# A graph network on one core: the attention sum fetches each visited tile's queries, and the experts' weights are split there instead of in the message sum

## The chip, the cores and the metric

The kernel runs on 1 core of a Trainium2 chip. The metric is the device time of one execution in microseconds (us). Times are compared as medians of several runs.

## The reference, cut to what matters

The model is two layers over 3125 nodes with 256 features and 50,000 edges (sorted by destination). A layer adds a message sum over the graph, a mixer and a feed-forward block, and layer 1 has an attention over the edges. The two parts that matter here:

```
# layer 0: messages along the edges (a scaled sum per destination node)
x = x + gnn(xn, W, edges) + mix(xn)
# layer 1: attention over the edges, 8 heads of 32
q = feat @ Wq.T + bq;  k = feat @ Wk.T + bk;  v = feat @ Wv.T + bv
score = clip(sum(q[edge_dst] * k[edge_src]) / sqrt(32), -10, 10)      # per edge and head
alpha = softmax of score over the edges of one destination
wv = segment_sum(alpha * v[edge_src], edge_dst)
# end of layer 1: a shared expert and 8 routed ones (top 2 of 8)
shared = gelu(x @ W1s + b1s) @ W2s + b2s
priv   = gelu(x @ W1p[e] + b1p[e]) @ W2p[e] + b2p[e]
```

The experts' weights W1p (8 x 256 x 1024), W2p (8 x 1024 x 256), W1s and W2s are float32. The kernel uses them as two float16 halves, a high one and the rest, which it makes itself and keeps in DRAM (`wsplit`) until the expert stage at the end.

## The kernel before, in words

The program is a row of phases with a barrier of all engines behind each (`phase`, L105 and L115). The nodes are 25 tiles of 125 rows (`T`, `R`). The edges are 80 groups of 5 x 125 (`G`, `J`). As the edges are sorted by destination, a group touches only one to a few node tiles; each (group, tile) pair is a *visit*, and `group_table` tells every engine the first tile, the number of tiles and the number of visits before a group (`group_bounds`, L522).

**Message sum** (`message_sum`, L686). For each group GpSimd issues 5 indirect DMAs (L750), each of which gathers 125 source rows of 1 KB (two float16 halves) into one of 4 slots. For each visit VectorE builds a one-hot matrix (L773), TensorE sums the gathered rows into the tile with it (L811), and VectorE adds the sum to the node tile (`Adder.add`, L557). VectorE also copies the next group's indices for GpSimd (L784). Two jobs ride along. The `Turner` transposes other weights in five parts. The `Splitter` (L628) works through 18 half-experts: SyncE issues two loads of 512 KB (L660), ScalarE makes the high float16 halves (L676), VectorE the low ones (L681, after every second group, for the first 18 of 20 turns of the loop), and SyncE stores two results of 512 KB (L664).

**Attention sum** (`attention_sum`, L1632). At its start SyncE issues one load of all queries, 3.2 MB, into the buffer of `m.y` (L1705), and then, for each group, a load that spreads the group's 625 destination numbers over 125 partitions, 312.5 KB (L1709), two buffers ahead. GpSimd gathers, per group, 5 x 125 rows of 2 KB (key and value, L1689) into one of 5 slots. For each visit ScalarE makes one-hot columns (L1736, L1742), four visits ahead at most (`PICKS`), and TensorE picks each edge's query out of the tile with 10 matmuls (L1784, between three that clear and three that close the bank, L1775 and L1788). VectorE multiplies queries and keys and reduces them to scores (L1822, L1827, L1828), ScalarE takes the exponential (L1749), VectorE weighs the values (L1834) and builds the one-hots of the sum (L1866), TensorE sums (L1810), VectorE adds to the tile (L555). TensorE picks for group n+2 before it sums group n. After the loop VectorE waits for the last gathers and divides by the sums (L1878 to L1883).

The order on each engine is the program's, written out by hand; semaphores tie the engines. SyncE and ScalarE each have a DMA queue of their own for the loads and stores they issue, GpSimd has the one of the gathers.

Of the kernel before, what the change touches and what calls it, by code (L numbers as in the profile page):

```python
# [25 lines left out]
C = 256  # L26
CB = C // 128
R = 125
# [599 lines left out]
class Splitter:  # L628
# [20 lines left out]
    def move(self, sp, e, h):  # L649

        i = e * 2 + h
        source, at = (self.shared, h) if isinstance(e, int) else (self.own, i)
        for s in range(2):
            sp.wait_ge(self.s_whole[s], i + AHEAD)
# [5 lines left out]
            sp.dma_start(to, taken).then_inc(self.s_raw[s], 16)  # L660
        rows = self.m.wsplit[:, :, 0:WALL].rearrange("e p (k l h n) -> e p k l h n", k=2, l=2, h=2)
        for s in range(2):
            sp.wait_ge(self.s_whole[s], i + 1 + AHEAD)
            sp.dma_start(rows[bass.ds(e, 1), :, :, s, h, :].rearrange("e p k n -> p (e k) n"),  # L664
                         self.split[:, s, :, :].rearrange("p k n -> p (k n)").bitcast(F32)
                         .rearrange("p (k n) -> p k n", k=2)).then_inc(self.s_stored[s], 16)

    def finish(self, sp):
        for s in range(2):
            sp.wait_ge(self.s_stored[s], self.steps * 16 + AHEAD)  # L670
# [15 lines left out]
def message_sum(nc, m, a):  # L686
# [6 lines left out]
    with phase(nc, "ms") as ph:  # L693
# [11 lines left out]
        splitter = Splitter(nc, m, a, ph)  # L705
        splitter.s_pace = s_pace
        PARTS = 5
        each = G // SLOTS // PARTS
        whole = splitter.steps

        def stretches(part):

            lo, hi = part * each, (part + 1) * each
            cuts = sorted({lo, hi, *([whole] if lo < whole < hi else [])})
            return list(zip(cuts, cuts[1:]))

        with nc.Block() as block:

            @block.sync
            def _(sp):  # L720
                with sp.Fori(0, X8) as e:
                    for h in range(2):
                        splitter.move(sp, e, h)
                for h in range(2):
                    splitter.move(sp, X8, h)
                splitter.finish(sp)

# [28 lines left out]
            def _(dve):  # L756
# [7 lines left out]
                def groups(i, splits):  # L764

                    for s in range(SLOTS):
# [18 lines left out]
                        if splits and s % 2:  # L785
                            splitter.low(dve, i, s // 2)
                    return before + count

                with dve.Fori(0, whole) as i:
                    groups(i, True)  # L790
                with dve.Fori(whole, G // SLOTS) as i:
                    visits = groups(i, False)
                adder.finish(dve.snap(visits), s_pace)
# [838 lines left out]
def attention_sum(nc, m, dst):  # L1632
# [9 lines left out]
    with phase(nc, "as") as ph:  # L1642
# [10 lines left out]
        q16 = m.y[:, :, :].rearrange("p t c -> p (t c)").bitcast(F16).rearrange("p (t k c) -> p t k c", t=T, k=2)  # L1653
# [6 lines left out]
        zeros = ph.sb("zeros", [R, R], F16)  # L1660
# [4 lines left out]
        summed = ph.sb("summed", [R, T, W])  # L1665
# [9 lines left out]
        ph.ahead(s_pick, *[s_total, s_added] * LAG)  # L1675
        ph.ahead(*[s_pickv] * PICKS)
        with nc.Block() as block:
# [25 lines left out]
            @block.sync  # L1703
            def _(sp):
                sp.dma_start(q16.rearrange("p t k c -> p t (k c)"),  # L1705
                             m.gather_q.rearrange("(t p) n -> p t n", p=R)).then_inc(s_q, 16)

                def load(g, s):
                    sp.dma_start(dsts[:, s, :],  # L1709
                                 dst[bass.ds(g * (J * R), J * R)].unsqueeze(0).broadcast_to([R, J * R]))\  # L1710
                        .then_inc(s_dst[s], 16)

                for s in range(2):
                    load(s, s)
# [5 lines left out]
                for g in range(G, GP):  # L1720
                    sp.wait_ge(s_dfree, g - 1)
                    load(g - G, g % 2)

            @block.scalar
            def _(act):
# [30 lines left out]
                one_hots(2, 1, 0, group_bounds(act, m, 2))  # L1756
                with act.Fori(0, G // (2 * SLOTS)) as i:
                    for s in range(2 * SLOTS):
                        n = i * (2 * SLOTS) + s
                        bounds = group_bounds(act, m, n + 3)  # L1760
                        weights(n + 1, (s + 1) % SLOTS)
                        one_hots(n + 3, i * SLOTS + (s + 3) // 2, (s + 3) % 2, bounds)

            @block.tensor
            def _(pe):
                def pick_q(g, bounds):
# [5 lines left out]
                    anything = q16[:, 0, :, :].rearrange("p k c -> p (k c)")  # L1772
                    for b in range(3):
                        n = min(512, J * C - b * 512)
                        pe.matmul(picked[:, b, 0:n], zeros[:, :], anything[:, 0:n], start=True, stop=False)  # L1775
                    with pe.Fori(0, count) as k:
                        visit = pe.snap(before + k)
                        tile = pe.snap(nc.s_assert_within(first + k, 0, T - 1))
                        pe.wait_ge(s_pick, visit + 1 + AHEAD)
                        pe.sem_inc(s_pace, 1)  # L1780
                        for j in range(J):
                            at = j % 2 * C
                            for p in range(2):
                                ins = pe.matmul(picked[:, j // 2, at:at + C], pick[:, visit % PICKS, j * R:(j + 1) * R],  # L1784
                                                q16[:, tile, p, :], start=False, stop=False)
                        ins.then_inc(s_pickv, 1)
                    for b in range(3):
                        ins = pe.matmul(picked[:, b, 0:1], zeros[:, :], anything[:, 0:1], start=False, stop=True)  # L1788
                    ins.then_inc(s_picked, 1)

                pe.wait_ge(s_q, 16)
# [23 lines left out]
            def _(dve):  # L1815
# [1061 lines left out]
def graph_layers(nc, a, out):  # L2877
    m = Memory()
    with ExitStack() as stack:
# [83 lines left out]
        attention_sum(nc, m, a["dst"])  # L2963
# [25 lines left out]
```

## Time and profile before

| | |
|---|---|
| median of 3 runs | 3982.84 us (3981.74 to 3984.69) |
| the profiled execution | 3987.43 us, its span 3985.7 us |
| busy: PE, DVE, ACT, POOL | 65%, 54%, 32%, 33% |
| mean granted TensorE clock | 0.807 of full speed |
| moved by DMA | 373 MB, mean 94 GB/s |
| message sum | from 235 to 889 us of the span |
| attention sum | from 2369 to 3133 us of the span |

In the profile PE is TensorE, DVE is VectorE, ACT is ScalarE, POOL is GpSimd and SP is SyncE; PEld is the loading of TensorE's weights. A name like SPq is the engine's instruction queue, which issues DMAs. "Idle before" is the time in which an engine did nothing ahead of an instruction, with what ended it; "issue" means that nothing the profile shows was waited for. "DMA share" is the mean busy share of the core's 16 DMA engines, so a transfer that keeps 4 of them busy shows as 0.25.

### The profile page before, as it was taken

Reading aid. Unit: us, or ns where it says so; the run is one execution under the profiler, and the core shown is the slowest. Engines: PE = TensorE matmul, PEld = TensorE weight load, DVE = VectorE, ACT = ScalarE, POOL = GpSimd, SP = SyncE. Lnnn points to the kernel's source line nnn. Section 1 sums busy time; section 2 is a strip of 40 time slices with the busy share of each in tenths; the row PEclk is TensorE's granted clock in tenths of the full one; section 3 lists DMA queues with packets and bytes.
Section 4 is the critical chain, followed back from the end, with each engine's and each line's share of the span. In section 5 each row is a group of like instructions: output and inputs, shape, how many; then the busy total and the mean of one; then the engine's idle time right before and its main releaser. Section 6 shows DMA issues by size and latency. Waiting matters only on the chain. (4 is left out here: it accounts for less than half of the span.)

```text
span 3985.7 us, 66521 instructions
## 1 busy us (share of the span) xinstructions
PE 2587.3 (65%) x17122; PEld 2086.2 (52%) x17123; DVE 2170.5 (54%) x4408; ACT 1269.1 (32%) x2467; POOL 1315.5 (33%) x1017
## 2 busy tenths in 40 slices
PE   4413333436678699996375434777777487699997
PEld 4413333323367477774254423555555366589986
DVE  6523333322456388885237764777777555544445
ACT  0300010003143255553257732222222243345441
POOL 0048888853000000000001024888888500211115
PEclk9855555557679599997597767999999778699998
DMA  1046666730000000001200015777777200356643
GB/s 36 32 105 157 156 165 162 197 94 6 0 22 0 16 11 13 16 16 46 73 0 0 0 40 150 193 189 187 189 191 189 52 21 0 124 188 229 227 159 91
DMA packets 255391, 373.00 MB, mean 94 GB/s; under 512 B 119009, under 2 KB 180889, under 8 KB 250965
## 3 DMA queue, kind: packets, MB, share of 16 engines
q0 software_dynamic: 154752, 174.53, 18.2%
q1 hardware_dynamic: 87700, 185.50, 14.2%
q10 hardware_dynamic: 12864, 12.06, 1.1%
q8 instruction: 37, 0.61, 0.1%
q14 instruction: 38, 0.30, 0.0%
HBM read 320.09 MB, written 50.96 MB: 93 GB/s over the span
## 5 line engine op out<-in xcount | busy, mean ns | idle before, releaser
L750 POOL DMA_INDIRECT ms_got<-gather,ms_index x400 | 506.2, 1265 | 124.9 <-issue 114.4
L1689 POOL DMA_INDIRECT as_gkv<-gather_kv,as_index x340 | 462.0, 1359 | 108.7 <-issue 100.9
L811 PE MATMUL ms_total<-ms_got,ms_hot 125*125 125x256 f16 x1040 | 231.0, 410 | 376.8 <-DMA ms_got<-gather,ms_index 251.9
L811 PEld LDWEIGHTS ms_total<-ms_got,ms_hot 125*125 x1040 | 202.9, 219 | 405.0 <-issue 405.0
L2097 POOL MEMSET bm_fx<- 128x128 f32 x1 | 0.2, 205 | 1013.0 <-POOLq L115 1013.0
L1810 PE MATMUL as_total<-as_gkv,as_hot 125*125 125x264 f32 x850 | 218.8, 406 | 78.0 <-DVE as_summed L555 65.6
L1478 ACT ACTIVATE ex_h<-ex_up,ex_now 128x313 f32<-128x313 f32 (+1 forms) x320 | 196.1, 613 | 197.2 <-PE ex_up L458 190.0
L1810 PEld LDWEIGHTS as_total<-as_gkv,as_hot 125*125 125x125 f32 x850 | 157.7, 193 | 117.8 <-issue 91.8
L2791 DVE CAST moe_hidden<-moe_h 128x256 f16<-128x256 f32 (+1 forms) x336 | 101.8, 303 | 209.9 <-ACT moe_h L2728 209.3
L2728 ACT ACTIVATE moe_h<-moe_up,moe_w 128x256 f32<-128x256 f32 (+1 forms) x336 | 163.1, 487 | 135.2 <-PE moe_up L458 93.2
L1784 PE MATMUL as_picked<-y_rows,as_pick 125*125 x1060 | 150.3, 291 | 52.6 <-issue 47.7
L2680 PE MATMUL moe_down<-moe_w,moe_hidden 128*128 128x256 f16 x1536 | 178.1, 273 | 0.0
L458 PE MATMUL moe_up<-moe_cols,moe_w 128*128 128x256 f16 x1536 | 172.9, 273 | 1.4 <-ACT moe_cols L2735 1.4
L1784 PEld LDWEIGHTS as_picked<-y_rows,as_pick 125*125 x1060 | 123.9, 141 | 87.3 <-issue 84.5
L2567 POOL DMA_INDIRECT moe_rows<-gather,moe_taken x64 | 63.0, 984 | 309.9 <-PE moe_turned L2655 259.8
L676 ACT ACTIVATE ms_split<-ms_raw 128x1024 f16<-128x1024 f32 x36 | 37.6, 1054 | 390.8 <-DMA ms_raw<-in_L_ffn_W1p 350.0
L1520 DVE TENSOR_TENSOR ex_h<-ex_h 128x313 f16<-128x313 f32 (+1 forms) x320 | 155.4, 486 | 11.0
L458 PEld LDWEIGHTS moe_up<-moe_cols,moe_w 128*128 128x128 f16 x1536 | 150.2, 98 | 19.0 <-issue 1.6
L2680 PEld LDWEIGHTS moe_down<-moe_w,moe_hidden 128*128 128x128 f16 x1536 | 150.4, 98 | 17.3
L1866 DVE SCALAR_TENSOR_TENSOR as_hot<-row_no,as_node,edge_dst 125x625 f32<-125x625 f32 x104 | 90.6, 871 | 120.5 <-issue 61.7
L2793 DVE TENSOR_TENSOR moe_hidden<-moe_h,moe_hidden 128x256 f16<-128x256 f32 (+1 forms) x336 | 148.3, 441 | 11.6
L458 PE MATMUL ex_down<-ex_w,ex_h 128*125 128x256 f16 x1200 | 148.1, 276 | 2.3
(448 smaller groups left out, 5895.2 us busy)
## 6 DMA issues: line engine op xcount, KB each, us to landing
moe_w<-wsplit SPq DMA_DIRECT2D x34, 2052.0 KB
as_dsts<-in_dst SPq DMA_DIRECT2D x83, 305.2 KB
wsplit<-ms_split SPq DMA_DIRECT2D x36, 512.0 KB
ms_raw<-in_L_ffn_W1p SPq DMA_DIRECT2D x16, 512.0 KB
ms_raw<-in_L_ffn_W2p SPq DMA_DIRECT2D x16, 512.0 KB
results<-moe_made SPq DMA_DIRECT2D x32, 256.0 KB, 8.2
ms_got<-gather,ms_index POOLq DMA_INDIRECT x400
gather_kv<-qkv_out SPq DMA_DIRECT2D x5, 1250.0 KB
```

Of the source, the lines that this page charges most:

```text
L458: ins = pe.matmul(out, left(k, b), right(n, b), start=(i == 0), stop=(i == len(todo) - 1))
L750: pool.indirect_dma_start(out=got[:, s, j, :], out_offset=None, in_=m.gather0, in_offset=bass.IndirectOffsetOnAxis(ap=index[:, s, j:j + 1] ...
L811: ins = pe.matmul(total[:, visit % RING, 0:C], hot[:, visit % RING, j, :], got[:, s, j, p * C:(p + 1) * C], start=(j + p == 0), stop=(j + ...
L1478: act.activation(h32[:, u % 4, 0:n], up[:, u % 4, 0:n], ACT.Relu, bias=now[:, 1, layer, o:o + 1], scale=now[:, 0, layer, o:o + 1]).then_in ...
L1520: dve.tensor_tensor(to[:, 1, o, at:at + n], full, to[:, 0, o, at:at + n], ALU.subtract).then_inc(s_h, 1)
L1689: pool.indirect_dma_start(out=gkv[s][:, j, 0:2 * C], out_offset=None, in_=m.gather_kv, in_offset=bass.IndirectOffsetOnAxis(ap=index[:, s, ...
L1784: ins = pe.matmul(picked[:, j // 2, at:at + C], pick[:, visit % PICKS, j * R:(j + 1) * R], q16[:, tile, p, :], start=False, stop=False)
L1810: ins = pe.matmul(total[:, visit % RING, 0:W], hot[:, s, j, :], gkv[s][:, j, C:C + W], start=(j == 0), stop=(j == J - 1))
L2680: ins = pe.matmul(down[:, h, 0:C], hidden[:, k, f, h * 128:(h + 1) * 128], part(s, r, 1, f, 0, C), start=False, stop=(f == FB - 1 and n == 2))
L2728: act.activation(h32[:, u % 4, 0:n], up[:, u % 4, 0:n], ACT.Gelu, scale=1.0 / WS, bias=bias(s, f)).then_inc(s_h32, 1)
L2791: dve.tensor_copy(hidden[:, 0, f, at:at + n], full).then_inc(s_hhigh, 1)
L2793: dve.tensor_tensor(hidden[:, 1, f, at:at + n], full, hidden[:, 0, f, at:at + n], ALU.subtract).then_inc(s_hidden, 1)
```

## The change

The queries are no longer loaded at the start. SyncE now walks the visits and, for each, waits until the fetch before it has landed and the slot is free, and then loads the visited tile's queries, 125 rows of 1 KB, into a ring of four (`queries`). TensorE waits for that load ahead of a visit's ten matmuls. The freed buffer takes the attention's running sums, so `m.y` becomes a view with a row of 264 elements in place of 256. The `Splitter` leaves the message sum: SyncE's program there is empty, and ScalarE and VectorE have no split work. In the attention sum ScalarE issues the loads and stores and makes the high halves at five points of its 10-group loop, VectorE makes two low halves after every fifth group, and the two half-steps of the shared expert follow after the loops. The diff, cut to its core:

```diff
-    def move(self, sp, e, h):
+    def load(self, act, e, h):
...
+    def store(self, act, e, h):
+        i = e * 2 + h
...
-            @block.sync
-            def _(sp):
-                with sp.Fori(0, X8) as e:
-                    for h in range(2):
-                        splitter.move(sp, e, h)
-                for h in range(2):
-                    splitter.move(sp, X8, h)
-                splitter.finish(sp)
-                    for lo, hi in stretches(part):
-                        if hi <= whole:
-                            with act.Fori(lo, hi) as i:
-                                for s in range(2):
-                                    splitter.high(act, i, s)
...
-                        if splits and s % 2:
-                            splitter.low(dve, i, s // 2)
...
-        q16 = m.y[:, :, :].rearrange("p t c -> p (t c)").bitcast(F16).rearrange("p (t k c) -> p t k c", t=T, k=2)
+        q16 = ph.sb("q16", [R, PICKS, 2, C], F16)
...
-        summed = ph.sb("summed", [R, T, W])
+        summed = m.y_wide
+        splitter = Splitter(nc, m, a, ph)
...
-                sp.dma_start(q16.rearrange("p t k c -> p t (k c)"),
-                             m.gather_q.rearrange("(t p) n -> p t n", p=R)).then_inc(s_q, 16)
...
+                def queries(g):
+                    first, count, before = group_bounds(sp, m, g)
+                    with sp.Fori(0, count) as k:
+                        visit = sp.snap(before + k)
+                        tile = sp.snap(nc.s_assert_within(first + k, 0, T - 1))
+                        sp.wait_ge(s_q, visit * 16 + AHEAD)
+                        sp.sem_inc(s_pace, 1)
+                        sp.wait_ge(s_pickv, visit + 1)
+                        sp.sem_inc(s_pace, 1)
+                        sp.dma_start(q16[:, bass.ds(visit % PICKS, 1), :, :].rearrange("p a k c -> p (a k c)"),
+                                     m.gather_q[bass.ds(tile * R, R), :]).then_inc(s_q, 16)
                 with sp.Fori(0, G // 2 - 1) as i:
                     for s in range(2):
+                        queries(i * 2 + s)
                         sp.wait_ge(s_dfree, i * 2 + (s + 1))
                         load(i * 2 + (s + 2), s)
...
+                splits = {0: lambda e: splitter.load(act, e, 0), 2: lambda e: high(e, 0),
+                          4: lambda e: (splitter.store(act, e, 0), splitter.load(act, e, 1)),
+                          6: lambda e: high(e, 1), 8: lambda e: splitter.store(act, e, 1)}
+                def high(e, h):
+                    for k in range(2):
+                        splitter.high(act, e * 2 + h, k)
...
+                        if s in splits:
+                            splits[s](i)
+                for h in range(2):
+                    splitter.load(act, X8, h)
+                    high(X8, h)
+                    splitter.store(act, X8, h)
+                splitter.finish(act)
...
-                        tile = pe.snap(nc.s_assert_within(first + k, 0, T - 1))
+                        pe.wait_ge(s_q, visit * 16 + (16 + AHEAD))
...
-                                                q16[:, tile, p, :], start=False, stop=False)
+                                                q16[:, visit % PICKS, p, :], start=False, stop=False)
...
+                        if s == 3:
+                            for k in range(2):
+                                splitter.low(dve, i, k)
                 adder.finish(dve.snap(before + count), s_pace)
+                for h in range(2):
+                    for k in range(2):
+                        splitter.low(dve, X8 * 2 + h, k)
...
-            m.y = y_stack.enter_context(nc.sbuf_tensor(f"y_rows{turn}", [R, T, C], F32))
+            m.y_wide = y_stack.enter_context(nc.sbuf_tensor(f"y_rows{turn}", [R, T, C + X8], F32))
+            m.y = m.y_wide[:, :, 0:C]
```

## Rows read from the trace of the kernel before

**Rows 1.** Page, part 4: the chain that ended last, by line, shares of the span.

```profile
PE moe_up L458 5%; PE moe_down L2680 4%; PE moe_down L2642 1%; DVE moe_hidden L2793 1%; DVE x_rows L2829 0%; DVE moe_hidden L2791 0%; PE moe_turned L2655 0%; PE moe_down L2675 0%; POOL z_rows L2577 0%; DMA moe_w<-wsplit 0%; DVE z_rows L2809 0%; DMA z_rows<-results,place 0%; DVE rowvec L2806 0%; PE moe_down L2694 0%; DVE x_rows L2820 0%
```

**Rows 2.** Groups by line, GpSimd, 237 to 872 us: count, busy, mean, idle before.

```profile
L750 POOL DMA_INDIRECT ms_got<-gather,ms_index x400 | 506.2, 1265 | 124.9 <-issue 114.4 <-DVE ms_index L784 7.6 <-DVE ms_index L761 2.9
```

**Rows 3.** Groups by line, GpSimd, 2435 to 3115 us.

```profile
L1689 POOL DMA_INDIRECT as_gkv<-gather_kv,as_index x320 | 437.7, 1368 | 102.3 <-issue 94.6 <-DVE as_index L1840 7.8
L1689 POOL DMA_INDIRECT z_flat<-gather_kv,as_index x80 | 110.2, 1377 | 63.9 <-DVE as_index L1840 39.7 <-issue 24.2
```

**Rows 4.** Line 750's instructions: duration min, median, max; the low halves' groups.

```profile
L750 POOL DMA_INDIRECT ms_got<-gather,ms_index x400: 1206/1214/2237, 237.6 to 864.5; - x134
...
L681 DVE SCALAR_TENSOR_TENSOR ms_split<-ms_raw,ms_split 128x1024 f16<-128x1024 f32 x36 | 44.1, 1226 | 3.8 <-ACT ms_split L676 3.1
```

**Rows 5.** Timeline, attention sum's start, all engines: start, length, [idle before].

```profile
2368.82 0.29 SPq L1705 DMA_DIRECT2D y_rows<-gather_q  x1
2398.97 1.21 POOL L1689 DMA_INDIRECT as_gkv<-gather_kv,as_index  x1 [0.31 <-issue]
2422.08 1.32 PE L1775 MATMUL as_picked<-y_rows,as_zeros 125*125 125x512 f16 x3 [63.12 <-DMA y_rows<-gather_q]
2424.78 0.82 ACT L1736 ACTIVATE z_flat<-as_dsts,as_minus_node 125x625 bf16<-125x625 int32 x1 [59.69 <-DMA as_dsts<-in_dst]
2429.91 1.49 DVE L1822 TENSOR_TENSOR z_flat<-as_picked,as_gkv 125x1280 f32<-125x1280 f32 x1 [51.61 <-PE as_picked L1788]
```

**Rows 6.** Windows: stretch, its length, busy of five engines, clock, DMA share, GB/s.

```profile
2373.00:2400.00 27.00, 0.00 (x0) 0.00 (x0) 4.88 (x2) 0.00 (x0) 21.64 (x18) 0.50 0.82 203
2408.00:2419.00 11.00, 0.00 (x0) 0.00 (x0) 0.00 (x0) 0.00 (x0) 0.00 (x0) 0.50 0.34 115
2500.00:3000.00 500.00, 357.07 (x1921) 271.13 (x1920) 374.46 (x454) 139.98 (x213) 406.47 (x297) 0.98 0.75 190
300.00:363.00 63.00, 21.89 (x100) 19.23 (x99) 20.18 (x33) 4.23 (x4) 51.07 (x40) 0.58 0.57 145
810.00:860.00 50.00, 17.95 (x80) 15.88 (x80) 13.46 (x25) 0.00 (x0) 39.91 (x34) 0.53 0.34 85
755.00:775.00 20.00, 8.53 (x40) 6.80 (x41) 2.86 (x5) 3.79 (x5) 16.02 (x14) 0.59 1.07 295
```

**Rows 7.** DMA issues of the whole span: count and KB (1024 bytes) of each.

```profile
as_dsts<-in_dst SPq DMA_DIRECT2D x83, 305.2 KB
...
y_rows<-gather_q SPq DMA_DIRECT2D x1, 3125.0 KB
```

**Rows 8.** Instructions of line 1784: ten matmuls for each visit.

```profile
L1784 PE MATMUL as_picked<-y_rows,as_pick x1060: 272/273/446, 2427.2 to 3101.2; 125*125 x177
```

**Rows 9.** Waits of VectorE and ScalarE in the attention sum: total, times, longest.

```profile
DVE z_flat L1822 <- DMA as_gkv<-gather_kv,as_index: 20.1, 13, 3.5
ACT as_gkv L1749 <- DVE as_score L1828: 320.8, 64, 8.2
```

**Rows 10.** Timeline, message sum: one half-step's issue, landing and halves.

```profile
584.95 0.37 SPq L660 DMA_DIRECT2D ms_raw<-in_L_ffn_W1p  x1
591.97 1.06 ACT L676 ACTIVATE ms_split<-ms_raw 128x1024 f16<-128x1024 f32 x1 [26.23 <-DMA ms_raw<-in_L_ffn_W1p]
594.42 1.06 ACT L676 ACTIVATE ms_split<-ms_raw 128x1024 f16<-128x1024 f32 x1 [1.39 <-DMA ms_raw<-in_L_ffn_W2p]
```

**Rows 11.** Timeline, the end of the attention sum.

```profile
3107.31 0.43 DVE L555 TENSOR_TENSOR as_summed<-as_summed,as_total  x1 [2.85 <-PE as_total L1810]
3113.10 1.21 POOL L1689 DMA_INDIRECT as_gkv<-gather_kv,as_index  x1 [0.31 <-issue]
3121.01 0.36 DVE L1878 TENSOR_SCALAR as_gkv<-as_summed 125x200 f32<-125x200 f32 x1 [13.27 <-DMA as_gkv<-gather_kv,as_index]
```

**Rows 12.** Timeline, attention sum at the full clock and at the low one.

```profile
2440.77 2.48 PE L1810 MATMUL as_total<-as_gkv,as_hot 125*125 125x264 f32 x10
3102.76 4.17 PE L1810 MATMUL as_total<-z_flat,as_hot 125*125 125x264 f32 x10 [1.18 <-DVE as_hot L1866]
```

More of the change, by code:

```diff
@@ L659, in move, with finish @@
                 to = self.raw[:, 1, :].rearrange("p (b n) -> p b n", n=C)
-            sp.dma_start(to, taken).then_inc(self.s_raw[s], 16)
+            act.dma_start(to, taken).then_inc(self.s_raw[s], 16)
+    def store(self, act, e, h):
+        i = e * 2 + h
         rows = self.m.wsplit[:, :, 0:WALL].rearrange("e p (k l h n) -> e p k l h n", k=2, l=2, h=2)
         for s in range(2):
[L663 to L668, printed above, removed]
+            act.wait_ge(self.s_whole[s], i + 1 + AHEAD)
+            act.dma_start(rows[bass.ds(e, 1), :, :, s, h, :].rearrange("e p k n -> p (e k) n"),
+                          self.split[:, s, :, :].rearrange("p k n -> p (k n)").bitcast(F32)
+                          .rearrange("p (k n) -> p k n", k=2)).then_inc(self.s_stored[s], 16)
+    def finish(self, act):
         for s in range(2):
-            sp.wait_ge(self.s_stored[s], self.steps * 16 + AHEAD)
+            act.wait_ge(self.s_stored[s], self.steps * 16 + AHEAD)
     def high(self, act, i, s):
@@ L704, in message_sum @@
         turner = Turner(nc, m, a, ph)
-        splitter = Splitter(nc, m, a, ph)
-        splitter.s_pace = s_pace
         PARTS = 5
         each = G // SLOTS // PARTS
[L709 to L715, printed above, removed]
-        with nc.Block() as block:
-            @block.sync
-            def _(sp):
-                with sp.Fori(0, X8) as e:
-                    for h in range(2):
-                        splitter.move(sp, e, h)
-                for h in range(2):
-                    splitter.move(sp, X8, h)
-                splitter.finish(sp)
+        with nc.Block() as block:
             @block.scalar
@@ L762, in _ @@
                 adder = Adder(nc, dve, "ms", m.x, total, s_total, s_added, m.inv_sqrt_degree)
-                def groups(i, splits):
+                with dve.Fori(0, G // SLOTS) as i:
                     for s in range(SLOTS):
@@ L784, in groups @@
                         dve.tensor_copy(index[:, free, :], nxt).then_inc(s_index, 1)
-                        if splits and s % 2:
-                            splitter.low(dve, i, s // 2)
[L787 to L793, printed above, removed]
+                adder.finish(dve.snap(before + count), s_pace)
             @block.tensor
@@ L1674, in attention_sum @@
         s_hot, s_total, s_added, s_pace, s_v = (ph.sem(x) for x in ("hot", "total", "added", "pace", "v"))
-        ph.ahead(s_pick, *[s_total, s_added] * LAG)
+        splitter.s_pace = s_pace
+        ph.ahead(s_pick, s_q, *[s_total, s_added] * LAG)
         ph.ahead(*[s_pickv] * PICKS)
@@ L1720, in _ @@
                 for g in range(G, GP):
+                    queries(g - 2)
                     sp.wait_ge(s_dfree, g - 1)
                     load(g - G, g % 2)
+                queries(GP - 2)
             @block.scalar
@@ L1771, in pick_q @@
                         pe.sem_inc(s_pace, 1)
-                    anything = q16[:, 0, :, :].rearrange("p k c -> p (k c)")
                     for b in range(3):
                         n = min(512, J * C - b * 512)
-                        pe.matmul(picked[:, b, 0:n], zeros[:, :], anything[:, 0:n], start=True, stop=False)
+                        pe.matmul(picked[:, b, 0:n], zeros[:, 0:R], zeros[:, 0:n], start=True, stop=False)
                     with pe.Fori(0, count) as k:
                         visit = pe.snap(before + k)
-                        tile = pe.snap(nc.s_assert_within(first + k, 0, T - 1))
+                        pe.wait_ge(s_q, visit * 16 + (16 + AHEAD))
+                        pe.sem_inc(s_pace, 1)
                         pe.wait_ge(s_pick, visit + 1 + AHEAD)
@@ L1784, in pick_q @@
                                 ins = pe.matmul(picked[:, j // 2, at:at + C], pick[:, visit % PICKS, j * R:(j + 1) * R],
-                                                q16[:, tile, p, :], start=False, stop=False)
+                                                q16[:, visit % PICKS, p, :], start=False, stop=False)
                         ins.then_inc(s_pickv, 1)
                     for b in range(3):
-                        ins = pe.matmul(picked[:, b, 0:1], zeros[:, :], anything[:, 0:1], start=False, stop=True)
+                        ins = pe.matmul(picked[:, b, 0:1], zeros[:, 0:R], zeros[:, 0:1], start=False, stop=True)
                     ins.then_inc(s_picked, 1)
-                pe.wait_ge(s_q, 16)
                 pe.wait_ge(s_zero, 2)
@@ L2962, in graph_layers @@
         take_y(1)
[L2963 removed]
+        attention_sum(nc, m, a)
         attention_out(nc, m)
```

7 lines of the change are left out of this document (4 added, 3 removed).

## The prediction

> **What bounds the kernel now.** I read first the chain of waits, then each changed stage by itself. The chain that ended last [rows 1] lies in the expert stage, which the change doesn't touch; every stage ends at a barrier, so what the two changed stages gain or lose goes straight into the time.
>
> The message sum is bound by GpSimd issuing gathers. 400 of them take 1265 ns and sit idle 125 us in all, nearly all "issue" [rows 2]: 506 + 125 = 631 of the 635 us from 237 to 872. The transfers, ScalarE and VectorE have room.
>
> The attention sum looks the same: from 2435 to 3115 GpSimd issues 400 gathers in 437.7 + 110.2 + 102.3 + 63.9 = 714 us, and of its idle time only 39.7 + 7.8 us wait for an index, 39.7 of it once, at the start [rows 3]. Without that it is 674 us for 80 groups, 8.43 us per group. The reader is to keep the second question open, though: how near to full are the DMA engines, and which of them?
>
> **The change part by part.**
>
> *Split work out of the message sum.* SyncE, ScalarE and DMA weren't late there, so only what slows GpSimd's issue counts. A gather's median is 1214 ns against a mean of 1265 [rows 2, 4]: 0.051 x 400 = 20 us is lengthening. The 36 low halves (44 us of VectorE, 1226 ns each) and 91 us of one-hots are what it can come from. None or all of the 20 us could be the halves'; I take half, a gain of 10 us.
>
> *The start of the attention sum.* The load of all queries is issued at 2368.8 and TensorE starts at 2422.1; VectorE's first scores come at 2429.9, while GpSimd has been out of slots since 2400.2 [rows 5]. With one tile to fetch behind two small loads I put VectorE's first scores near 2385: 45 us earlier, and GpSimd's stall of 39.7 us goes.
>
> *The fetches and the splits as traffic.* This is the term that decides. From 2408 to 2419 nothing but the query load runs, with a backlog, and the DMA share is 0.34 at 115 GB/s [rows 6]: 0.34 x 16 = 5.4, about five of the 16 engines. The load of destination numbers that is issued right behind it reaches ScalarE only at 2424.8, after 59.7 us of waiting [rows 5]: it stood in the queue of the same five. From 2373 to 2400, with gathers beside the load, the share is 0.82, or 13 engines, so gathers use the other engines too, and I spread them evenly. All loads into 125 partitions on SyncE's queue then fall on one set of five engines: the load of destination numbers, and the new fetches.
>
> By the Trainium skill ("DMA: Bandwidth & Descriptors", "Why a DMA increments its semaphore by 16 and not by 1") a load from SyncE or ScalarE uses the largest number of engines up to 16 that divides its rows, and always the lowest-numbered; 125 rows give 5. The trace's 5.4 agrees, and by the rule the fetches speak against this change.
>
> Work on each of those five, in us:
> - a gather. Three readings. At the start 20 gathers put 20 x 5/16 = 6.25 on an engine, taking five engines for each; the query load of 3.2 MB [rows 7] needs 3200/115 = 27.8 us alone and took 53.3; less an estimated 4 for issue and landing, 21.5/6.25 = 3.4. In the message sum's last turns 0.34 x 50 x 16 / 34 / 5 = 1.6 for rows half as long, so 3.2. In the steady attention sum 0.75 x 500 x 16 = 6000 engine-us, less 59 loads of destinations x 13.5, over 297 gathers and five: 3.5 [rows 6]. I take 3.3.
> - a load of destinations: 312.5 KB at 115 GB/s, 2.7.
> - a fetch: 1/25 of 3.2 MB, 1.11, once per visit; there are 1060/10 = 106 visits [rows 8], 1.3 per group.
> - a half-step of the split, 2.1 MB over all 16 engines: the share is 0.57 with it and 0.34 without [rows 6], and 63 us hold two, so 0.23 x 63 / 2 = 7.2.
>
> Per group the five carry 5/16 x 5 x 3.3 + 2.7 = 7.9 us now, 93% of 8.43: nearly full, though the mean share is 0.75. VectorE already waits 20.1 us for gathers [rows 9]. After: 7.9 + 1.3 x 1.11 + 7.2/5 = 10.7 us per group. The whole stage: 131 x 3.3 + 83 x 2.7 + 106 x 1.11 + 16 x 7.2 = 433 + 224 + 118 + 115 = 890 us. Busy shares count waiting too: the mean reaches 1.07 where three queues run [rows 6], so 890/1.07 = 832 is the lower bound of this sum. I take 850, nearer to it, as this stage will also have three queues. The last gather lands at 2371 + 850 = 3221, not at 3121.
>
> *Instructions added.* ScalarE gets 32 high halves of 1.06 us and 64 issues of about 0.4; it idles 320.8 us on scores, 5.0 per group [rows 9], and hides them. A landing late for the high half stops its exponentials, and VectorE behind them; it has two groups to land, about 17 us, against 7.0 and 9.5 in the message sum [rows 10]. VectorE gets 32 low halves, 39 us; they hide under its waits for transfers. If the DMA weren't late they would show (rival A). SyncE waits for one landing per visit; behind it stand only the next destinations, two groups ahead.
>
> *The tail.* After the last add, at 3107.3, VectorE now waits 13.7 us for the last gathers, then divides from 3121.0 [rows 11]. The shared expert's two half-steps go there. ScalarE starts the first about 4 us before the last add; each takes 9.5 for landing [rows 10], 1.1, 1.2 and about 0.7 of semaphores, 12.5; so the division starts 25 - 4 = 21 us after the last add. The last add comes 13.7 us ahead of the last landing, at 3207; the division starts at 3228: 107 us later than before. If the landings cost nothing the tail costs 0, and 12 if they take half as long again.
>
> **The sum.** 3987.4 (the profiled execution; span 3985.7) - 10 + 107 = 4084. That execution is 4.6 above the median, so 4080. With 810 to 890 us of work: 4040 to 4120.
>
> **Rivals.**
>
> *A: the engines interleave better than they were charged, and GpSimd stays the bound: faster.* For it: the gathers kept 1214 ns with a backlog at the start, the steady stage waits little for transfers. Against: the 3.2 to 3.5 us come from three places. GpSimd: -39.7 for the stall, +11 for the low halves (400 gathers at 1.370 against 1.214 are 62 us long already [rows 3]; 32 of 36 halves cost what I took off above; 0 to 39), +10 for the coupling, as VectorE's chain gets as long: 3107.3 - 2429.9 - 20 + 39 + 5 = 701 from 2385 is 3086, and GpSimd's end is 3114.3 - 39.7 + 11 = 3086. The tail adds 21 - 13.7 = 7, the message sum gives 10: -22, so 3961. It decides if the five engines' work is below about 715 us (3086 less 2371), which by the same count needs a gather of 2.3 us: (715 x 1.07 - 457)/131.
>
> The Trainium skill ("SBUF — State Buffer", on the bandwidth-pool intuition) gives 358 GB/s from HBM to a core. By that the stage, at 190 + 50 + 20 = 260 GB/s of demand, would not be bound by transfers, which is A's time; 190 is the trace's, and no run here shows this stage at 358.
>
> *B: the fetches are late by their own order.* The next is issued only when the last has landed, and stands behind 2.7 us of destinations. If each of the 26 second visits of a group shows 2 us, on A's ground: -22 + 52, 4013. For it: a wait in the chain of every visit; against: SyncE is two groups ahead.
>
> *C: on top of the forecast TensorE loses its clock.* It runs at 0.98 in the steady stage and at 0.5 to 0.6 in the message sum [rows 6], where it is 35% busy. With groups of 850/84 = 10.1 us it falls from 71% to 59% busy. A sum of ten matmuls takes 4.17 in place of 2.48 [rows 12]; at half speed TensorE needs 6.0 x 1.7 = 10.2 us per group, as long as the transfers; coupled, 30 to 60 more, 4120.
>
> **Chances.** Forecast 60%, A 22%, B 10%, C 8%. The range holds the forecast, B, C in part and A's edge: 3962 to 4135; the likeliest's own is 4040 to 4120. A measurement of this kernel tells 0.2%, 8 us, from no change. Faster: A but for its slow side, 21%. Within: 5%. Slower: 74%.
>
> **What would show it.** The message sum about 625 us long, with gathers at 1.24. VectorE's first scores near 2375, the message sum's 10 us included. Groups of about 10.1 us in the attention sum, GpSimd idle for indices by over 100 us, VectorE and TensorE waiting for gathers and fetches, a DMA share of about 0.8 at 215 GB/s. Wrong if GpSimd's idle time there is still nearly all "issue", or if a stage of over 760 us shows no wait for a transfer.

## The result: slower, and by more than the range allowed

| | before | after |
|---|---|---|
| median | 3982.6 us (3981.7 to 3984.7, 4 runs) | 4160.3 us (4157.5 to 4162.2, 4 runs) |
| ratio | 1 | 1.0445 [1.0427, 1.0463] |
| profiled execution | 3987.4, span 3985.7 | 4162.2, span 4160.5 |

Forecast: 4080, range up to 4135. The sign and the cause named, late transfers in the attention sum, came out as predicted. The size is 80 us short, and the time lies 25 us outside the range.

### The profile after

The page, parts 4 and 5 (the chain's engines; groups with their count, busy time, mean, and idle time before them):

```profile
PE 11%; DVE 2%; DMA 0%; POOL 0%; issue 0%; ACT 0%; DVEq 0%; POOLq 0%; ACTq 0%
...
L1663 POOL DMA_INDIRECT as_gkv<-gather_kv,as_index x340 | 470.9, 1385 | 291.2 <-DVE as_index L1843 200.0
L730 POOL DMA_INDIRECT ms_got<-gather,ms_index x400 | 498.9, 1247 | 125.1 <-issue 111.5
...
L1788 PE MATMUL as_picked<-as_q,as_pick 125*125 x1060 | 186.3, 339 | 212.4 <-DMA as_q<-gather_q 175.3
```

The chain still lies in the expert stage [rows 1] and says nothing about the change. The message sum's 400 gathers fell from 1265 to 1247 ns [rows 2]: 7 us, where 10 were forecast. In the attention sum the kind of wait has changed: GpSimd, which sat idle on indices for 39.7 + 7.8 us [rows 3], now waits 200.0 us for them, and TensorE, which waited for queries only once before, at the start, waits 175.3 us for fetches.

The waits of the attention sum after, 2364 to 3300 us (total, times, longest):

```profile
ACT as_gkv L1737 <- DVE as_score L1831: 454.8, 64, 18.6
...
POOL as_gkv L1663 <- DVE as_index L1843: 200.0, 42, 14.9
PE as_picked L1788 <- DMA as_q<-gather_q: 175.3, 44, 12.7
DVE as_hot L1869 <- PE as_total L1813: 130.2, 24, 14.6
DVE z_flat L1825 <- PE as_picked L1792: 110.6, 22, 14.1
...
DVE z_flat L1825 <- DMA as_gkv<-gather_kv,as_index: 21.4, 5, 11.1
```

SyncE's own longest wait, in the same stretch, is the one for the landing of the last fetch:

```profile
SPq L1694 <- DMA as_q<-gather_q: 513.7, 99, 13.2
```

Read from the transfer upwards: a fetch is late for TensorE (175), so the picked queries are late for VectorE (111), so the score is late for ScalarE (455 against 320.8 [rows 9]), so slots come free late and GpSimd has no index (200). VectorE hardly waits for gathers: 21.4 us, and 9.9 in the slots that the trace calls `z_flat`, against 20.1 and 3.4 before. So it is the fetches that were late, and not the gathers.

A window after (busy of PE, PEld, DVE, ACT, POOL, then granted clock, DMA share, GB/s), and the last add, the shared expert's low halves and the division on VectorE:

```profile
2500.00:3000.00 500.00, 315.43 (x1451) 247.79 (x1452) 303.90 (x363) 125.68 (x183) 314.26 (x226) 0.82 0.79 196
```

```profile
3270.10 0.43 DVE L555 TENSOR_TENSOR y_rows<-y_rows,as_total  x1 [1.13 <-PE as_total L1813]
...
3293.03 1.22 DVE L684 SCALAR_TENSOR_TENSOR as_split<-as_raw,as_split 128x1024 f16<-128x1024 f32 x1 [7.32 <-ACT as_split L679]
...
3295.61 0.35 DVE L1887 TENSOR_SCALAR as_gkv<-y_rows 125x200 f32<-125x200 f32 x1
```

Against [rows 6]: 226 gathers in the 500 us instead of 297, at nearly the same share and rate, 0.79 and 196 GB/s against 0.75 and 190. The division starts at 3295.6 instead of 3121.0 [rows 11], 174.6 later; from there to the span's end it is 864.9 us in place of 864.7. The whole loss lies ahead of the division.

One number per kernel carries the experiments: the time from the first to the last reduction of a score on VectorE. It contains neither the stage's start nor its tail. In the trace before and the trace after:

```profile
L1827 DVE TENSOR_REDUCE as_score<-z_flat x81: 1485/1486/1489, 2431.4 to 3098.9; 125x40 f32<-125x1280 f32 x81
```

```profile
L1830 DVE TENSOR_REDUCE as_score<-z_flat x81: 1486/1486/1487, 2383.6 to 3263.4; 125x40 f32<-125x1280 f32 x81
```

667.5 us before, 879.8 after. In the kernel before, 20 gathers are already issued when the scores begin; a kernel that starts early without the change takes 690 (below). Each length comes from one trace. The traced execution lies up to 9 us from its kernel's median (e1), so differences of lengths are good to some 10 us, and no better.

### The profile page after: what moved, and what is told of

It is laid out like the page before. It is cut to its first block and busy times, and to the rows that moved or that the text cites. A ratio compares the mean times of both kernels' runs of the same rounds, so it can differ in the third digit from the quotient of the medians.

```text
span 4160.5 us, 68233 instructions
## 1 busy us (share of the span) xinstructions
PE 2662.4 (64%) x17122; PEld 2157.0 (52%) x17123; DVE 2171.8 (52%) x4408; ACT 1266.3 (30%) x2467; POOL 1314.5 (32%) x1017
## 5 line engine op out<-in xcount | busy, mean ns | idle before, releaser
L1663 POOL DMA_INDIRECT as_gkv<-gather_kv,as_index x340 | 470.9, 1385 | 291.2 <-DVE as_index L1843 200.0
L730 POOL DMA_INDIRECT ms_got<-gather,ms_index x400 | 498.9, 1247 | 125.1 <-issue 111.5
L1788 PE MATMUL as_picked<-as_q,as_pick 125*125 x1060 | 186.3, 339 | 212.4 <-DMA as_q<-gather_q 175.3
L1813 PE MATMUL as_total<-as_gkv,as_hot 125*125 125x264 f32 x850 | 254.4, 455 | 53.5 <-DVE y_rows L555 49.0
L1788 PEld LDWEIGHTS as_picked<-as_q,as_pick 125*125 x1060 | 156.6, 169 | 245.4 <-issue 242.8
L1813 PEld LDWEIGHTS as_total<-as_gkv,as_hot 125*125 125x125 f32 x850 | 183.8, 226 | 101.8 <-issue 64.9
L616 ACT ACTIVATE ms_cols<-ms_bank 128x256 f32<-128x256 f32 (+2 forms) x26 | 11.7, 449 | 671.2 <-PE ms_bank L603 647.5
L1825 DVE TENSOR_TENSOR z_flat<-as_picked,as_gkv 125x1280 f32<-125x1280 f32 x65 | 96.7, 1488 | 121.7 <-PE as_picked L1792 100.2
L752 DVE SCALAR_TENSOR_TENSOR ms_hot<-row_no,ms_node,edge_dst 125x625 f32 x104 | 90.7, 872 | 133.1 <-issue 133.1
```

Source lines behind the costliest of these rows:

```text
L730: pool.indirect_dma_start(out=got[:, s, j, :], out_offset=None, in_=m.gather0, in_offset=bass.IndirectOffsetOnAxis(ap=index[:, s, j:j + 1] ...
L1663: pool.indirect_dma_start(out=gkv[s][:, j, 0:2 * C], out_offset=None, in_=m.gather_kv, in_offset=bass.IndirectOffsetOnAxis(ap=index[:, s, ...
L1813: ins = pe.matmul(total[:, visit % RING, 0:W], hot[:, s, j, :], gkv[s][:, j, C:C + W], start=(j == 0), stop=(j == J - 1))
L1825: dve.tensor_tensor(qk[:, :].rearrange("p (j c) -> p j c", j=J), picked[:, :, :].rearrange("p b c -> p (b c)")[:, 0:J * C] .rearrange("p ( ...
```

## The experiments

Each stands beside runs of the kernel before on its chip; brackets are 95% intervals of the ratio. "Length" is the score-to-score time of its trace.

| run | what it is | ratio | first score | length |
|---|---|---|---|---|
| e1 | fetches; splits in the message sum | 1.0132 [1.0073, 1.0192] | 2395.9 | 766.9 |
| e2 | after; destinations on ScalarE's queue | 1.0529 [1.0497, 1.0562] | 2374.9 | 923.5 |
| e3 | after; fetch of 128 rows | 1.0339 [1.0309, 1.0369] | 2377.2 | 842.4 |
| e4 | after; destinations into 128 rows | 1.0383 [1.0353, 1.0413] | 2371.5 | 866.1 |
| e5 | after; two groups' fetches under way | 1.0462 [1.0441, 1.0483] | 2375.0 | 890.5 |
| e6 | e1; two groups' fetches under way | 1.0152 [1.0132, 1.0173] | 2398.6 | 764.0 |
| e7 | before; queries in five pieces | 0.9975 [0.9965, 0.9985] | 2391.2 | 697.2 |
| e8 | after; e3 and e4 | 1.0244 [1.0222, 1.0266] | 2376.2 | 799.4 |
| e9 | before; fetches that nobody reads | 1.0223 [1.0197, 1.0248] | 2431.5 | 758.5 |
| e10 | e1; thin fetches | 0.9964 [0.9948, 0.9981] | 2389.9 | 706.0 |
| e11 | before; destinations into 128 rows | 0.9992 [0.9982, 1.0002] | 2434.5 | 659.3 |
| e12 | e7 and e11 | 0.9963 [0.9947, 0.9979] | 2397.7 | 690.8 |
| e13 | after; thin fetches | 1.0282 [1.0264, 1.0301] | 2378.2 | 826.4 |
| e14 | after; thin splits | 1.0247 [1.0219, 1.0276] | 2406.7 | 791.1 |
| e15 | after; both thin | 1.0101 [1.0079, 1.0124] | 2401.9 | 733.4 |
| e16 | before; pieces spread out | 0.9969 [0.9957, 0.9981] | 2389.7 | 690.3 |

### Is it the fetch, the split, or the order of the queue?

*e1, one half of the change.*

```diff
+ (message sum)   splitter.move / high / low, as in the kernel before
- (attention sum) splitter.load / high / low / store
```

> The splits go back into the message sum as before; the attention sum keeps the fetch of each tile's queries. Theory W (the five DMA engines that serve loads into 125 partitions have too much work; the changed kernel's stage took about the 890 us that the plain sum gives): the splits' 115 us leave those five engines and the tail's 12 us go, the message sum gets its 7 us back: about 4040 us. Theory O (each fetch waits for the landing of the last, and stands behind the destinations in one queue; the engines aren't full): the splits ride on another queue, so the fetches hardly get faster: above 4110 us.

4035.2 us, beside the 4040 of theory W. The fetch costs 52 net of the earlier start; moving the splits costs the other 125.

*e2, order alone: the destinations leave SyncE's queue.*

```diff
-    sp.dma_start(dsts[:, s, :], ...)       # between the fetches
+    act.dma_start(dsts[:, s, :], ...)      # behind the square that frees the slot
```

> The changed kernel with the loads of destination numbers issued by ScalarE on its own queue, right after the one-hots that free the buffer; SyncE's queue holds only the fetches. The same bytes on the same five engines. Theory W: no change, 4145 to 4170 us. Theory O: a fetch no longer stands behind 2.7 us of destinations, 106 times, so TensorE's waits for queries fall by more than half of their 175 us: below 4080 us.

4193.3, slower still. TensorE waits 190.2 us for fetches instead of 175.3, though nothing stands ahead of a fetch in its queue. The place behind the destinations isn't the cause.

*e5 and e6, the wait of one fetch for the last one's landing.* SyncE waited 513.7 us at that wait in the trace after, so it had to be tried.

```diff
-    s_q = ph.sem("q")
+    s_q = [ph.sem(f"q{s}") for s in range(2)]     # by the group's parity
...
+                    with pe.Fori(count, MOST) as k:       # TensorE's program, for each group: MOST is 4
+                        pe.sem_inc(s_q[par], 16)
```

> The changed kernel with one semaphore for each parity of the group, so that the fetches of two neighbouring groups may be under way together; the same bytes, buffers and queues. Theory C (new, from the four runs before: the stage is a chain of 106 fetches, each issued when the last has landed; in the changed kernel and the four runs a visit takes the fetch's time from issue to last byte plus 1.0 to 1.5 us): the chain opens, the stage falls to what bounds it next, 4000 to 4080 us. Theory W (the five engines are full): the same bytes take the same time, 4150 us or more.

> The splits in the message sum as before, the fetches of two groups under way together. Theory C: with the chain open the stage is bound by GpSimd's issue again and starts 45 us earlier: 3940 to 3965 us. Theory W: the five engines carry 775 us of work against about 715 us of issue by GpSimd: 4020 to 4040 us, as with one fetch at a time.

4166.8 and 4043.6: nothing gained, on either base. But the edit also puts a loop of semaphore instructions into TensorE's program, between a group's last pick and the matmuls that close its bank. TensorE's waits in e1, then in e6, 2362 to 3310 us:

```profile
PE as_picked L1799 <- DMA as_q<-gather_q: 111.7, 44, 6.5
```

```profile
PE as_picked L1807 <- issue: 78.3, 67, 1.5
...
PE as_picked L1801 <- DMA as_q<-gather_q: 29.6, 13, 4.8
```

TensorE's wait for fetches fell by 82 us, and 78 us came up ahead of the closing matmuls, where e1 has none. In e5 it is 99.4 in place of 175.3, and 62.9 new. So the two runs took one wait away and put about as much in, and they don't show that the wait was free. That each fetch waits for the last one's landing stays a possible part of the cost.

### Is it the traffic, or waiting for it?

*e9 has the traffic without TensorE's wait for it, e10 every wait without most of the traffic.* In e9 SyncE still waits for each landing, and the next destinations are issued behind it.

```diff
e9 (from before)
+    sp.dma_start(idle[:, visit % PICKS, ...], m.gather_q[tile * R : ...])   # never read
e10 (from e1)
-    sp.dma_start(q16[...],          m.gather_q[tile * R : ..., :])
+    sp.dma_start(q16[...][:, 0:64], m.gather_q[tile * R : ..., 0:64])
```

> The kernel before, queries held whole and splits in the message sum, and beside it each visit's fetch of 125 rows into a scratch ring that nobody reads: the traffic of the fetches without TensorE's wait for them. Theory W (the five engines' work): 118 us more on each of the five, no earlier start: 4070 to 4100 us. Theory D (what costs is that TensorE waits for a fetch): 3980 to 3995 us.

> As the first of these experiments (fetches in the attention sum, splits in the message sum), but each fetch takes only 64 of a row's 512 elements; the rest of the queries is left out (zero). Every wait, issue and landing stays, an eighth of the bytes. Theory W: the five engines carry about 680 us, GpSimd's issue bounds the stage and it starts 45 us earlier: 3940 to 3970 us. Theory D: 4025 to 4045 us, as with the whole rows.

4082.6 and 3978.9. Unread fetches lengthen the stage from 667.5 to 758.5, 91 us. The same fetches thinned to an eighth, with every wait in place, leave 706.0. Fetches cost by their bytes. Rows of the waits and windows, of e9 and of e10. e9 didn't get rid of waiting: ScalarE waits 405.4 us for destinations, where it waited 59.7 before, and SyncE 355.9 us for landings.

```profile
ACT z_flat L1757 <- DMA as_dsts<-in_dst: 405.4, 64, 60.4
...
SPq L1724 <- DMA z_flat<-gather_q: 355.9, 84, 8.4
...
2500.00:3000.00 500.00, 332.42 (x1685) 255.81 (x1685) 325.94 (x398) 124.26 (x189) 348.17 (x258) 0.91 0.70 182
```

```profile
PE as_picked L1803 <- DMA as_q<-gather_q: 43.6, 26, 4.7
...
2500.00:3000.00 500.00, 358.63 (x1863) 275.13 (x1861) 362.61 (x440) 137.28 (x209) 394.08 (x287) 0.94 0.74 185
```

Fewer bytes make a fetch land sooner and also leave the engines freer. These two runs don't tell one from the other.

### Is it the five engines, or all sixteen?

If 125 rows confine a load to five engines, 128 rows free it.

```diff
-    q16  = ph.sb("q16",  [R, PICKS, 2, C], F16)      # e3, e8
+    q16  = ph.sb("q16",  [128, PICKS, 2, C], F16)
-    dsts = ph.sb("dsts", [R, 2, J * R], I32)         # e4, e8, e11, e12
+    dsts = ph.sb("dsts", [128, 2, J * R], I32)
```

> The changed kernel, each fetch 128 rows into 128 partitions in place of 125 (three rows too many, not used), so 16 engines can share it. Theory W: the fetches' 118 us on each of the five become 37: about 4080 us. Theory O: the fetch itself gets 0.8 us shorter, 106 times, at its place behind the destinations: 4075 us at most gain, more likely 4110, as the wait ahead of it stays.

> The changed kernel with the destination numbers spread over 128 partitions in place of 125 (the last three are not read). Theory W: 224 us on each of the five become 72, so the five are no longer full and GpSimd or VectorE bounds the stage: 3990 to 4020 us. Theory O: a fetch stands behind 0.9 us in place of 2.7: 4060 us.

> The changed kernel with the fetches and the destination numbers both moved as 128 rows, one fetch at a time. Theory W: the work on the five engines falls from 890 to about 660 us, below GpSimd's 715: 3990 us. Theory C: a visit takes the fetch's time plus 1.3 us; with fetches of about 6.2 us that is 106 x 7.5 = 795 us against 893: 4060 us.

> The kernel before with the destination numbers spread over 128 partitions. If GpSimd's issue alone bounds its attention sum: no change, 3978 to 3990 us. If the five engines, 102% busy by their packets' times, bound it as well: 3955 to 3975 us.

4117.5, 4135.1, 4080.0, 3990.3. Each relief helps, 43, 25 and 80 us, far less than theory W had counted (80, at least 140, and 170). e3's time is nearer to theory O's 4110, and e8's 4080 nearer to theory C's 4060 than to W's 3990. e8's window:

```profile
2500.00:3000.00 500.00, 331.15 (x1610) 257.34 (x1609) 335.54 (x402) 138.95 (x202) 351.91 (x252) 0.88 0.95 220
```

The share is 0.95 at 220 GB/s: with the work spread, the mean over all sixteen is high. Spreading also costs. From the queue views of 2500 to 3000 us (share x 8000 engine-us over the count): e8 has 49 loads of destinations and 66 fetches at 23.0%, 1840 engine-us. The trace after has 45 and 59 at 15.0%, 1200. For each load of destinations, with its 1.3 fetches, that is 38 in place of 27. By the Trainium skill ("DMA: Bandwidth & Descriptors", "Why a DMA increments its semaphore by 16 and not by 1") 128 rows use sixteen engines where 125 use five. For 125 rows the 5.4 engines read from [rows 6] agree; no run shows a load of 128 rows alone. The gain is not in the ratio of 16 to 5. e11 shows that without the change there is nothing to relieve: the kernel before is bound by GpSimd, as [rows 3] said. That also says what a sum of packet times is worth. In the kernel before, gathers at 62.4% and destinations at 12.5% of 16 engines put 62.4 + 12.5 x 16/5 = 102% on each of the five, if gathers spread evenly; e11 lowers it to 58.1 + 17.1 = 75%, and the time doesn't move.

### What is each part worth? Two by two

*e13, e14, e15* keep every instruction and wait of the change and thin its transfers. Thin splits move a quarter of the bytes in and out (my expectation says an eighth out, wrongly). To have the rest of the weights defined, e14 and e15 store zeros in the message sum and clear a buffer, so their first gather comes at 2387.5 and 2385.3 in place of 2363.1; the length is free of that. As they leave out part of the data, e10 and e13 to e15 compute something else than the kernel does; they are for timing alone.

```diff
e13, e15:  the fetch as in e10
e14, e15:
-    source[0][at, :, :]                      to raw[:, 0, :]
+    source[0][at, :, 0:C]                    to raw[:, 0, 0:C]
-    act.dma_start(rows[e, :, :, s, h, :],    split[:, s, :, :])
+    act.dma_start(rows[e, :, 0:1, s, h, 0:C], split[:, s, 0, :])
```

> The changed kernel whole, but each visit's fetch moves 64 of its 512 elements per row (the rest of the tile is zero, so what is picked differs). Theory S (the stage takes the plain sum of the work of the five DMA engines): from 890 to 433 + 224 + 118/8 + 115 = 787 us, times 906/890 as measured, 801 in place of 906: about 4055 us (4045 to 4070), and the wait of TensorE for fetches falls from 175 to under 80 us. Theory O (the overlap that I divided by is real, and the added 80 us come from elsewhere: ScalarE's queue, the wait for a fetch): the traffic is worth 118/1.07 less what is hidden, and the stage is then bound by the splits' waits: above 4090 us.

> The changed kernel whole, but the splits in the attention sum load and store a quarter and less of their weights (256 of 1024 columns in, an eighth of the result out; the rest of the experts' weights is zero, stored in the message sum). ScalarE's and VectorE's instructions and all waits stay. Theory S: the splits' 115 us of the five engines fall to about 22: 95 us less, and the tail's landings are shorter: about 4055 us (4040 to 4075), and ScalarE's waits for split loads fall from 63 us to under 20. Theory I (the splits cost by their instructions and waits on ScalarE and VectorE, not by traffic): above 4120 us.

> Both at once: every instruction and every wait of the change, with an eighth of the fetches' bytes and under a fifth of the splits'. Theory S: the five engines carry 433 + 224 + 15 + 22 = 694 us, less than GpSimd's issue, so the stage is bound as before: earlier start -45, low halves +11, tail about +5: 3950 to 3990 us, and GpSimd waits under 60 us for indices. Theories O and I: above 4030.

4101.8, 4090.7, 4026.0, beside 3990 for the kernel before. All three lie above theory S's ranges (4045 to 4070, 4040 to 4075, 3950 to 3990). Some 22 to 24 us of that are the late start of e14 and e15, which leaves e14 inside and e15 14 us above. e13's time is the one that theory O had. Three lines of the traces, of e13, e14 and e15:

```profile
L1834 DVE TENSOR_REDUCE as_score<-z_flat x81: 1486/1486/1489, 2378.2 to 3204.6; 125x40 f32<-125x1280 f32 x81
```

```profile
L1843 DVE TENSOR_REDUCE as_score<-z_flat x81: 1486/1486/1487, 2406.7 to 3197.8; 125x40 f32<-125x1280 f32 x81
```

```profile
L1847 DVE TENSOR_REDUCE as_score<-z_flat x81: 1486/1486/1487, 2401.9 to 3135.3; 125x40 f32<-125x1280 f32 x81
```

| length, us | thin fetches | whole fetches | fetch bytes cost |
|---|---|---|---|
| splits in the message sum | 706.0 (e10) | 766.9 (e1) | 61 |
| thin splits | 733.4 (e15) | 791.1 (e14) | 58 |
| whole splits | 826.4 (e13) | 879.8 (after) | 53 |
| split bytes cost (whole less thin) | 93 | 89 | |
| thin splits cost | 27 | 24 | |

The rows and columns hardly interact. From the 690.3 of an early start without the change (e16): 690 + 16 (waits and the fetches' eighth) + 57 + 26 + 91 = 880, the length after. Theory S, "the plain sum of the five engines' work sets the time", holds for the splits: three quarters of their traffic, 86 us of the 115, came back as 89 to 93. It fails for the fetches: 103 us of counted work removed, 53 to 61 returned. Theory O, that a real overlap hides part of the traffic, fits that half; I (instructions and waits on ScalarE and VectorE) falls: 24 to 27 us, about what the quarter of traffic that was left is worth.

### The early start by itself

*e7, e12 and e16* take only what is good in the change: the first scores need one fifth of the queries, not all.

```diff
-    sp.dma_start(q16, all 25 tiles); load(0, 0); load(1, 1)
+    load(0, 0); piece(0); load(1, 1)       # pieces 1 to 4: behind each later load (e7, e12),
+                                           # behind every third (e16)
```

> The kernel before, its queries still held whole, but loaded in five pieces: the first between the loads of the first two groups' destinations, the others one by one behind the next destinations. No fetch per visit, splits in the message sum. Both theories: only the start's stall of some 40 us goes, and GpSimd's issue bounds the rest: 3940 to 3955 us. If the five engines were what bounds the stage before, it would stay at 3975 us or more.

> The queries whole in five pieces, the destination numbers over 128 partitions. With the pieces alone the first scores came 40 us earlier and the time fell by 10 us only. Theory W: the pieces' 28 us on the five engines fit in once the destinations are off them: 3940 to 3955 us. If something else took the 30 us: 3970 us as with the pieces alone.

> The kernel before, the queries whole in five pieces, but the four later ones are each sent behind every third load of destinations, and TensorE waits for each piece only ahead of the groups that may need it (in the first version it waited 31 us once for all four, and ScalarE 67 us for destinations behind them). If these two waits took the other 26 us of the 40 that the earlier start was worth, 3945 to 3960; if the early stretch is slow for its low TensorE clock or its gathers, 3965 to 3975 again.

3972.5, 3977.8 and 3975.8 beside 3982.4, 3992.1 and 3990.2: 10 to 14 us faster than the kernel before, all three, and the only versions that do the whole work and beat both kernels. (They rely on the edges being sorted by destination: the first groups read the first tiles.) The first score comes 34 to 42 us earlier, and about two thirds of it are lost again; the 3940 to 3955 of e7 and e12 were missed. e12 takes the destinations off the five engines as well and gains no more than e16, which speaks against those engines as what takes it back. My reading for e16 was wrong: the 31 us of TensorE that I put down to the later pieces are its first wait of the stage. e16 still has it, and it gained no more:

```profile
ACT z_flat L1745 <- DMA as_dsts<-in_dst: 55.9, 11, 17.6
PE as_picked L1784 <- DMA y_rows<-gather_q: 29.9, 1, 29.9
```

GpSimd saves only 16 us of waiting for indices: 25.7 + 5.7 = 31.4 us, in place of 39.7 + 7.8 = 47.5. From 2400 to 2500 e16 issues 49 gathers where the steady stage issues 59, at a granted clock of 0.83 and with destinations late. Which of the two, clock or transfers, makes that stretch slow stays open.

## Why the prediction was wrong by 80 us, step by step

- *What bounds the kernel*: right. GpSimd was the bound: e11 finds no change when the five engines are relieved. That there was little room beside it e9 shows, with 91 us more when they are loaded.
- *Message sum, -10*: 7. Right.
- *The start*: the first score at 2383.6 where about 2375 was forecast. GpSimd's stall at the start went, as said, but e16 shows that an early start isn't worth its 45 us.
- *The stage's transfers, the step that failed*: "890/1.07 = 832 ... I take 850, nearer to it". From the first gather (2363.1) to the last add (3270.1) it is 907 us, where 850 less 13.7 was forecast: 71 of the missing 80. Dividing by 1.07 was 40 of them. The 1.07 is a share of busy time from 20 us of another stage [rows 6], and it was used as if it made engines faster. The other 31 are what the stage took beyond the plain sum itself: 907 + 14 = 921 to the last landing, by the forecast's own 13.7, against 890. The sum's terms were too small too. By the queue shares of 2500 to 3000 us, before: 59 loads of destinations at 12.5% of 8000 engine-us, 16.9 each, 3.4 on each of five engines where I took 2.7; after: 226 gathers at 50.3%, 3.6 where I took 3.3; 59 fetches in what is left of 15.0%, 1.5 where I took 1.1; splits at 13.5%, about 8 for a half-step where I took 7.2. Those together make 131 x 3.6 + 83 x 3.4 + 106 x 1.5 + 16 x 8 = 1041 us in a stage of 907. So packets of several queues do overlap, and time per packet grows as they do; neither number is the engine's work. What the runs show in its place are the parts' costs in the table above: 57 us for seven eighths of the fetches' bytes, 91 for three quarters of the splits' and 26 for the rest of the splits. Whether they come from five full engines, or from fetches that land late and are issued one at a time, stays open. Two things speak for the second. SyncE, which waited 477.4 us for ScalarE before, waits 70.7 for it now and 513.7 for landings; and the gathers, which use the same engines, weren't late.
- *Max or sum*: I let the first 58 us of added transfers (715 less 657) vanish under GpSimd's issue. e1 over e16 is 77 us for 118 of counted work, so some 40 vanished; after over e1 is 113 for 115, so nothing did of the splits.
- *Instructions*: right. ScalarE's and VectorE's halves are hidden; e15 bounds them.
- *The tail*: 3295.6 - 3270.1 = 25.5, forecast 21. ScalarE waits 9.8 and 7.5 us there for the two first landings; [rows 10] had 7.0 and 9.5 from issue to use. Right within its bounds.
- *Signs*: gathers at 1247 (1240 forecast), GpSimd idle for indices 219 us (over 100), DMA share 0.79 (0.8), 196 GB/s (215), groups of 11.0 us (10.1), TensorE waiting for fetches. The one that missed is VectorE waiting for gathers.
- *The rivals*: A falls (four runs at 4157 or more). A's own sum is 2 us off: 32 of 36 halves of the 10 us are 9, and not 11. B's wait is there, 513.7 us of SyncE, and the argument against it, that SyncE is two groups ahead, failed; what it costs is open, as e5 and e6 put another wait in its place. C came in part: TensorE's clock is 0.82 in the stage against 0.98 [rows 6], which is a result of its waits: thin transfers bring it back to 0.93 (e15) without a change to TensorE's work. From the first gather to the last add the same 2592 matmuls keep TensorE busy for 562.9 us in place of 487.4, so up to 75 us of the loss could pass through the clock. What it costs by itself wasn't separated.

## What to carry to other kernels

Before work is moved under a stage that seems bound by one engine's issue, count what each DMA engine already carries there, by the rows of each load: here the mean share was 0.75, and 106 small loads that nobody read cost 91 us. Add the new traffic in full, at packet times read in that stage rather than from a load running alone, and give no credit for an overlap seen elsewhere. Such a sum warns; it is not a bound, as e11 shows. To find the price of a transfer, thin its bytes and keep its waits: two such knobs, alone and together, took the loss apart. And look at what a counter-experiment adds: e5 and e6 removed one wait and brought in another as long.

## What the runs showed of the hardware

- Spreading loads from 125 to 128 rows raised the share from 0.79 to 0.95 and the rate only from 196 to 220 GB/s (e8): for a load of destinations with its 1.3 fetches 38 engine-us instead of 27. Taking a relief of 16/5 for granted made me overrate e3 by 37, e4 by 115 at least and e8 by 90 us.
- Added transfers cost time at a mean share well under 1: e9 lost 91 us at 0.70, below the 0.75 of the faster kernel before. The costs of fetches and splits add up within the 10 us to which the lengths are good.
- The bytes of the splits (loads and stores of 512 KB) cost what was counted for them, 89 to 93 us for 86, those of the fetches (125 KB) about half, 53 to 61 for 103. Why isn't shown by these runs.
